# Bias as a product in the graph convolutions, residual biases on VectorE, and another list of steps

## The reference

```python
# layer 2: three graph convolutions, biases b1, b2, b3
support = jnp.einsum('bnf,fh->bnh', x, W)
return jnp.einsum('bnm,bmh->bnh', adj, support) + b     # relu behind the first two
# layer 3: attention over 8 heads of 64, then the adjacency terms
attn = jax.nn.softmax(dots, axis=-1) * LA
attn = attn + LG * adj + LD * jnp.exp(-dist)
return out @ W_out + b_out
```

## Time and profile before

| | us |
|---|---|
| median of 3 runs | 2879.51 (2878.45 to 2879.76) |
| the profiled execution | 2871.73 |
| its span, first to last instruction | 2869.9 |
| PE busy | 2666.2 (93%) |
| DVE busy | 1791.0 (62%) |
| ACT busy | 873.7 (30%) |
| POOL busy | 660.5 (23%) |

### The profile page before, as it was taken

The page is one execution under the profiler, slowest core; times in us unless marked ns, Lnnn a source line. Parts: engine busy times, 40 slices in busy tenths (PEclk is TensorE's granted clock), DMA queues, the critical chain, the costliest instruction groups (busy, mean ns, idle before and its releaser), DMA issues.

```text
span 2869.9 us, 73766 instructions
## 1 busy us (share of the span) xinstructions
PE 2666.2 (93%) x30296; PEld 2209.6 (77%) x30296; DVE 1791.0 (62%) x3498; ACT 873.7 (30%) x2397; POOL 660.5 (23%) x1005
## 2 busy tenths in 40 slices
PE   4999999999999999399999999999999999999998
PEld 2778878778877777387787788788788788778777
DVE  3778877887888887354654654654654554555465
ACT  2222222222222222332332332332333233233233
POOL 0222222222222222112212221220320320321221
PEclk9999999999999999699999999999999999999999
DMA  5011111111111110201101100100110110110000
GB/s 179 28 39 35 35 35 38 36 36 37 41 41 35 35 38 26 90 5 34 38 12 26 38 20 19 38 28 11 38 32 7 37 35 8 34 37 11 28 31 16
DMA packets 130004, 99.41 MB, mean 35 GB/s; under 512 B 89104, under 2 KB 91152, under 8 KB 129808
## 3 DMA queue, kind: packets, MB, share of 16 engines
q1 hardware_dynamic: 129808, 96.30, 11.2%
HBM read 62.68 MB, written 33.55 MB: 34 GB/s over the span
## 4 chain that ended last, share of the span: by engine, by line
PE 47%; DVE 6%; issue 3%; ACT 2%; SPq 1%; POOL 1%; DMA 0%; DVEq 0%; POOLq 0%
PE qs L1110 39%; PE qs L1141 4%; ACT E L975 2%; PE qs L1172 1%; PE qs L1151 1%; DVE Z L1090 1%; DVE sm L1016 1%; PE qs L1179 1%; DVE E L1070 1%; DVE Z L1085 1%; PE qs L1186 1%; DVE E L1074 0%; DVE E L1059 0%; DVE sm L1061 0%; ACT H L955 0%
## 5 line engine op out<-in xcount | busy, mean ns | idle before, releaser
L1110 PE MATMUL qs<-hi,T2h 128*128 128x512 f32 x1024 | 431.8, 422 | 14.1 <-DVE T2l L1013 14.1
L1110 PE MATMUL qs<-lo,T2h 128*128 128x512 f32 x1024 | 415.4, 406 | 0.0
L1110 PE MATMUL qs<-hi,T2l 128*128 128x512 f32 x1024 | 414.3, 405 | 0.0
L1013 DVE TENSOR_TENSOR T2l<-qs,T2h 128x512 fp32r<-128x512 f32 x320 | 212.4, 684 | 208.9 <-ACT T2h L951 115.8
L864 POOL TENSOR_SCALAR sm<-sm 128x1 f32<-128x1 f32 x128 | 29.9, 233 | 1279.4 <-DVE sm L1018 1279.4
L1110 PE MATMUL qs<-T2h,WQh 128*128 128x256 f32 x1024 | 293.3, 286 | 0.0
L1110 PE MATMUL qs<-T2l,WQh 128*128 128x256 f32 x1024 | 290.2, 283 | 0.0
L1110 PE MATMUL qs<-T2h,WQl 128*128 128x256 f32 x1024 | 290.2, 283 | 0.0
L1110 PEld LDWEIGHTS qs<-hi,T2h 128*128 128x128 f32 x1024 | 200.0, 195 | 64.7 <-DVE T2l L1013 17.0
L1110 PEld LDWEIGHTS qs<-hi,T2l 128*128 128x128 f32 x1024 | 199.9, 195 | 47.7
L1110 PEld LDWEIGHTS qs<-lo,T2h 128*128 128x128 f32 x1024 | 200.7, 196 | 40.9
(11 more groups left out here) (175 smaller groups left out, 5492.7 us busy)
## 6 DMA issues: line engine op xcount, KB each, us to landing
X<-in_x SPq DMA_DIRECT2D x64, 256.0 KB, 6.6
x<-R SPq DMA_DIRECT2D x64, 256.0 KB, 2.0
X<-x SPq DMA_DIRECT2D x64, 256.0 KB, 2.7
out<-Z SPq DMA_DIRECT2D x64, 256.0 KB, 2.1
AB<-in_adj SPq DMA_DIRECT2D x512, 8.0 KB, 1.5
A<-in_adj SPq DMA_DIRECT2D x128, 32.0 KB, 2.5
An<-in_adj SPq DMA_DIRECT2D x16, 128.0 KB, 2.2
WB<-in_adj SPq DMA_DIRECT2D x32, 64.0 KB, 7.2
```

The lines of the kernel that those rows point to most:

```text
L1013: return dve.tensor_tensor(lo, ps, hi.bitcast(F32), ALU.subtract)
L1110: mm = pe.matmul(out, lhsT, rhs, start=i == 0, stop=i == len(terms) - 1)
```

## The change

In `convolutions_and_attention`:
- The biases of g0 and g1 become a thirteenth product. Two tensors `brow` hold b1 and b2 split in two: rows 0 to 63 the hi part, rows 64 to 127 the lo part. `pick` is zero but for rows 0 and 64, which are one. pick-transposed times brow gives the bias in every row; it is the first product of the group and PE adds the twelve others to it. ACT then does relu straight from PSUM into H; DVE's adds (L1039) go.
- b3 and bo move from POOL to DVE.
- The addition of epsilon moves from POOL to DVE, behind the statistics; POOL keeps the power.
- Ahead of the first round POOL fills `first_rows`, ACT copies it and the bias rows, and DVE subtracts to get the lo parts. ACT waits for the bias loads ahead of its first splits, POOL no longer does.
- A new list. Its branch stands between av.1+ and wo.0; nearly the whole round now bears a "+".

```diff
-                        act.wait_ge(b_ok[i], n[c])
-                        act.activation(H[:, c, :], H[:, c, :], ACT.Relu).then_inc(g_sb[i], 1)
+                        act.wait_ge(g_ps[i], n[c])
+                        act.activation(H[:, c, :], psB[c][:, :], ACT.Relu).then_inc(g_sb[i], 1)
...
+            act.wait_ge(rows_ok, 2)
+            act.copy(pick[:, :], first_rows[:, :]).then_inc(pick_ok, 1)
+            act.wait_ge(bias_in, 4 * 16)
+            for row, raw_row in zip(brow, (b1_all, b2_all)):
+                act.copy(row[:, :], raw_row[:, :]).then_inc(brow_hi, 1)
...
-            def stats(src, c, n, bn, mv):
+            def stats(src, c, n, bn, mv, ve):
                 dve.bn_stats(col(c, BN, 6), src).then_inc(bn, 1)
                 alone(bn, n[c])
                 dve.bn_aggr(col(c, MV, 2), col(c, BN, 6)).then_inc(mv, 1)
+                alone(mv, n[c])
+                dve.tensor_scalar(col(c, VE), col(c, MV + 1), EPS, None, ALU.add).then_inc(ve, 1)
...
-                        dve.wait_ge(g_ps[i], n[c])
-                        dve.tensor_tensor(H[:, c, :], psB[c][:, :], (b1_all, b2_all)[i][:, :], ALU.add).then_inc(b_ok[i], 1)
+                    if step == "b3":
+                        dve.wait_ge(t_ps[0], n[c])
+                        dve.tensor_tensor(X[:, c, :], X[:, c, :], b3_all[:, :], ALU.add).then_inc(b3_ok, 1)
+                    if step == "bo":
+                        dve.wait_ge(xp_ps, n[c])
+                        dve.tensor_tensor(X[:, c, :], X[:, c, :], bout_all[:, :], ALU.add).then_inc(bo_ok, 1)
...
-                terms = []
+                terms = [] if row is None else [(pick[:, :], row[:, :])]
```

The list's new first and last lines (the old ones stand in the kernel above):

```diff
+            "wo.0 z4.0 wo.1 rs4.0 sm.2 x4.0 at.0+ ta.2 t0.0+ b3.0+ av.2 z4.1 rs4.1 sm.3 g0.0+ wo.2 ta.3 x4.1 t0.1+ av.3 z4.2 "
...
+            "s.0+ s.1+ sm.0+ sm.1+ qk.1+ ta.0+ ta.1+ av.0+ s.2+ s.3+ av.1+")
```

More of the change, by code:

```diff
@@ L710, in convolutions_and_attention @@
         mhalf = sb("mhalf2", [P, 1])
+        first_rows, pick = sb("first_rows", [P, P]), sb("pick", [P, P], F32R)
+        brow = [sb(f"brow{i}", [P, D], F32R) for i in range(2)]
         ln_ld = sb("ln_ld", [P, 1])
@@ L741, in convolutions_and_attention @@
             "consts_ok2", "ident02", "blocks0", "bias_in", "split_hi2", "split_lo2"))
+        rows0, rows_ok, pick_ok, brow_hi, brow_ok = map(sem, ("rows0", "rows_ok", "pick_ok", "brow_hi", "brow_ok"))
         load_in = [sem(f"load2_in{i}") for i in range(KD)]
@@ L747, in convolutions_and_attention @@
         qk_ps, qk_sb = ([sem(f"{n}{b}") for b in range(4)] for n in ("qk_ps", "qk_sb"))
-        b_ok = [sem(f"b_ok{i}") for i in range(2)]
         t_ps, th, t_sb, g_ps, g_sb = ([sem(f"{n}{i}") for i in range(3)] for n in ("t_ps", "th", "t_sb", "g_ps", "g_sb"))
@@ L854, in _ @@
             pool.memset(ln_ld[:, :], LN_LD).then_inc(consts_ok, 1)
+            pool.memset(first_rows[:, :], 0.0).then_inc(rows0, 1)
+            pool.wait_ge(rows0, 1)
+            pool.memset(first_rows[0:1, :], 1.0).then_inc(rows_ok, 1)
+            pool.memset(first_rows[C:C + 1, :], 1.0).then_inc(rows_ok, 1)
+            pool.wait_ge(rows_ok, 2)
             def alone(sem, value):
@@ L859, in alone, with rstd @@
                 pool.wait_ge(sem, value)
[L861 to L865, removed]
+            def rstd(c, n, ve):
+                alone(ve, n[c])
                 return pool.tensor_tensor(col(c, RS), col(c, VE), mhalf[:, :], ALU.pow)
@@ L883, in cm @@
                 pool.tensor_tensor(Cm[:, :, :, :], Cm[:, :, :, :], MM[:, :, :, :], ALU.mult).then_inc(cm_ok, 1)
-            pool.wait_ge(bias_in, 4 * 16)
             def steps(entries, it, reg):
@@ L893, in steps @@
                         cm(each[ahead], loaded[ahead])
[L894 to L899, removed]
                     if step == "rs3":
-                        rstd(c, n, mv3, ve3).then_inc(rs3, 1)
+                        rstd(c, n, ve3).then_inc(rs3, 1)
                     if step == "rs4":
-                        rstd(c, n, mv4, ve4).then_inc(rs4, 1)
+                        rstd(c, n, ve4).then_inc(rs4, 1)
             steps(START, -1, number)
@@ L998, in _ @@
             dve.wait_ge(bias_in, 4 * 16)
+            for n, (row, raw_row) in enumerate(zip(brow, (b1_all, b2_all))):
+                dve.wait_ge(brow_hi, n + 1)
+                dve.tensor_tensor(row[C:P, :], raw_row[C:P, :], row[C:P, :].bitcast(F32), ALU.subtract).then_inc(brow_ok, 1)
             for n, (raw_piece, hi, lo) in enumerate(pieces):
@@ L1035, in steps @@
                         rest(by_graph(Tl, c), halves(c), by_graph(Th, c)).then_inc(t_sb[i], 1)
-                    if step in ("g0", "g1"):
-                        i = int(step[1])
-                        dve.wait_ge(g_ps[i], n[c])
-                        dve.tensor_tensor(H[:, c, :], psB[c][:, :], (b1_all, b2_all)[i][:, :], ALU.add).then_inc(b_ok[i], 1)
+                    if step == "b3":
[4 more added lines that the diff above has]
+                        dve.tensor_tensor(X[:, c, :], X[:, c, :], bout_all[:, :], ALU.add).then_inc(bo_ok, 1)
                     if step == "z3":
@@ L1044, in steps @@
                         dve.wait_ge(z3, n[c])
-                        stats(X[:, c, :], c, n, bn3, mv3)
+                        stats(X[:, c, :], c, n, bn3, mv3, ve3)
                     if step == "x3":
@@ L1086, in steps @@
                         dve.wait_ge(z4, n[c])
-                        stats(Z[:, c % 2, :], c, n, bn4, mv4)
+                        stats(Z[:, c % 2, :], c, n, bn4, mv4, ve4)
                     if step == "x4":
@@ L1115, in three, with project @@
                 return [(lh, rh), (lh, rl), (ll, rh)]
-            def project(out, c, W):
-                terms = []
+            def project(out, c, W, row=None):
+                terms = [] if row is None else [(pick[:, :], row[:, :])]
                 for k in range(KD):
@@ L1146, in steps @@
                         pe.wait_ge(t_sb[i], n[c])
-                        project(psB[c][:, :], c, GW[i]).then_inc(g_ps[i], 1)
+                        project(psB[c][:, :], c, GW[i], (brow + [None])[i]).then_inc(g_ps[i], 1)
                     if step == "xp":
@@ L1194, in _ @@
             pe.wait_ge(split_lo, len(pieces) + KD)
+            pe.wait_ge(pick_ok, 1)
+            pe.wait_ge(brow_ok, 2)
             steps(START, -1, number)
```

## The result

The changed kernel takes 2907.82 us (2906.48 to 2909.2, 4 runs) where the kernel before takes 2878.98 beside it: ratio 1.0103, 95% interval 1.0087 to 1.0119. It is 1% slower, where 1% faster was forecast: 2849, with a range up to 2872. The profiled execution has a span of 2905.1 us.

The account below looks back on a forecast made before the run. PE was taken as the bound, idle at the branch and a few waits. Per round -3.90 - 0.41 + 0.06 + 1.37 + 0.60 = -2.28, times 15 = -34.2, ends +4: 2841.5 profiled, 2849 us median, range 2825 to 2872.

Parts of the forecast that it names:

- PE's own 3.90: Old branch between g2.0 and t2.1: said to cost PE 3.90 us a round, all saved by moving it.
- rival A: Branch's price moves with it: PE pays 0.94 + 1.61 ahead of wo.0, round +0.3, 2889 us; chance 0.09.
- Branch: New branch between av.1 and wo.0: PE's gap there 0.31 us, read from the first half's loop.
- Clock: Low clock in the run of products behind av.2: +0.60 us a round, bounds 0 and +1.1.
- Stretch: Attention's end to the next tiles, ta.0 to g0.0: 14.4 us; with ta.3 14.9 against 14.86, +0.06 a round.
- the walk: Step-by-step timing from ta.0 to g0.0: wo.1 ends at 9.8, ta.2 waits about 1.75, g0.0 starts at 14.4.
- DVE's branch: DVE's loop branch, moved between av.1's rest and z4.0: costs 0.87 us there, with PE waiting for DVE.
- relu: Relu straight from PSUM: the 0.83 us wait before t1 goes; with new waits of 0.42, -0.41 a round.
- the places named as tight: t1.3, t2.3 (inputs ready just at their turn) and t0.3 (its x tile): no wait counted.
- Products and rest: Eight pick products a round cost 1.87 us, 0.5 back from joined runs: +1.37, bounds +0.9 and +1.9.
- Ends: Work outside the loop: +4 us in all; last wo.0 to the end 26.2 us against 23.2.
- The 7.8: Added from profiled execution to median: the earlier kernel's median 2879.51 is 7.8 us above its profiled 2871.73.

Follow-up runs that it names:

- a_g2: Changed kernel, same cyclic order, branch moved from ahead of wo.0 to behind g2.3, cm.0 a few steps sooner: 2822.27 us, 0.982 of the kernel before.
- b_g2: Kernel before, same cyclic order and arithmetic, only its branch moved from behind g2.0 to behind g2.3: 2817.52 us, 0.9813 of the kernel before.
- arith_g2: Kernel before's list with all of the changed arithmetic, branch moved behind g2.3: 2837.51 us, 0.9881 of the kernel before.
- b_wo: Kernel before, same cyclic order, only its branch moved from behind g2.0 to between s.3 and wo.0: 2877.25 us, 1.001 of the kernel before.

## Why the prediction was wrong

The step that failed is this one: "So PE's own 3.90 goes, and 0.31 comes in a place that I walk below." The old price went, though it was 3.47 a round in the mean and not 3.90, which one pair of rounds had given. The 0.31 came from the first half's branch, taken as the same boundary because long products follow there too. It is not the same: that loop is not fetched anew (no instruction packets), the second half's is. What hides a fetch is first of all the long work queued ahead of the branch, and ahead of wo.0 stand only short steps. The gap is 4.29 us in the mean. "It decides once PE's gap behind the branch exceeds 2.3 us" is what rival A said, and it had 0.09.

Its parts, in the order of the sum:
- *Branch.* 4.29 instead of 0.31: +3.98. Even A was too low, as it took the 0.94 and 1.61 of before for the full price. There 24 long products of the earlier trace rows stand ahead, and the first gap is 0.73 to 1.42 over fourteen rounds. The second, 1.42 to 1.90, comes after 40 short products behind the branch: what stands behind it counts as well.
- *Clock.* +0.60 was set for the runs behind av.2. Those take 5.90 to 5.94 us for 25 products in every round, the full level; the low clock came in wo.0 and wo.1, 24 products in 7.77 in the mean instead of 5.79: +2.0.
- *Stretch.* Walked 14.4, measured 19.06 in the round shown and 19.80 in the mean of fourteen (19.06 to 20.83), with the branch in it. In a_g2, without it, 13.77; the walk less its 0.87 for DVE's branch is 13.5. Its waits are there: g0.0 0.95 (1.0 said), g0.1 0.28 (0.27), and av.3 none. ta.2 waits 0.94 and not 1.75, as PE is late itself (in a_g2 it is 0.59), and the walk's wait of 0.45 before wo.1 is not there either. DVE's branch shows nowhere: DVE stood 5.20 for PE.
- *relu.* The wait before t1 is gone. New are 0.30 to 1.12 before t0.3 for its x tile, one of the places named as tight.
- *Products and rest.* a_g2's round is 100.69. The sum without the branch's 0.31, DVE's 0.87 and the clock's 0.60 gives 102.0 - 1.8 = 100.2: 0.5 off, about what 3.90 less 3.47 comes to.
- *Ends.* To the end from the last wo.0: 27.2 (26.2 said). The scaling takes 0.54 (0.51).
- *From profile to median.* The 7.8 added did not come: 2906.9 profiled, 2907.82 in the median.

A round is 106.45 - 102.0 = 4.45 over the prediction. The stretch is 19.80 - 14.4 = 5.4 over. Of these the gap makes 3.98. From the start of wo.0 to ta.2 it is 7.77 + 0.95 = 8.7 where the walk has 7.8: +0.9, the low clock less the two waits that shrank. Some 0.4 are spread over the rest. Outside the stretch the round is 1.0 below the prediction, 0.60 of it the clock that was set there. 15 times 4.45 is 67 us, and the spans differ by 65 (2905.1 against 2841.5 - 1.8).

Set against a well placed branch, the rest of the change is worth little either way: 0.9813 with nothing of it (b_g2), 0.9881 with the arithmetic alone (arith_g2), 0.982 with arithmetic and list (a_g2). By the medians the list wins back what the arithmetic costs; the intervals of the last two overlap (0.9852 and 0.9867), so this is likely and not shown. The place of the branch is worth 1.9% in before's cycle and some 2.8% in after's (0.982 / 1.0103, with cm.0 moved too).

## What to carry to other kernels

Look in the DMA view for instruction packets inside a loop. If there are any, the jump back can leave an engine without instructions: cut the cyclic order where that engine has its longest queued instructions just before the branch, never behind short ones. Look behind the branch too: before has 24 long products ahead of it and two short steps behind, and still paid 3.47 us a round; the good places have 36 long ones ahead and a single short step behind. A branch cost read from another loop may be used only if both loops fetch or both don't. And a gap of PE has a second price in the clock of the products behind it.

## What the runs showed of the hardware

- A branch back in a loop of 1847 or more counted PE instructions: 3.4 to 4.95 us of idle PE behind steps of short products, 1.8 to 2.5 behind products of 0.121 us, 0 to 0.37 behind 36 of 0.233. Behind 24 of 0.233 with short steps following: 0.73 to 1.42, and 1.42 to 1.90 more after 40 short products. At 1527: 0 to 0.54; at 1566: 0.31 to 0.36.
- How much is queued when the sequencer jumps stays open. If the same fetch is hidden by q products, a gap of 2.03 at 0.121 us each and of at most 0.37 at 0.233 give an estimate of at least 1.66 / 0.112 = 15. But if it were 15, 24 long products ahead would do as well as 36, and before's 0.73 to 1.42 say that they do not.
- The fetching itself shows no gap elsewhere in a round: in a_g2, besides the branch, PE has only some 0.2 us marked issue, before t0.0. About 11 packets of 16 KB a round come in before, after, a_g2 and b_g2 alike.
- After PE stood 4.7 us the granted clock was 0.50 for the next 5.28 us, then 0.97 (b_wo); after 4.0 us it was 0.80 in the mean over 8.35 us (after). In the round of a_g2 shown, with no idle time over 0.95 in the stretch, it stayed at 1.00.
- One cause can stand under two releasers: the same gap is put down to T2l in six rounds and to issue in eight, though in the round shown the T2l that wo.0 needs was there 4.3 us before PE went on.
